# Rotary tables of a layer built by ScalarE in two slots, and the stream of groups written out without a loop

## The reference

```python
x = L0_attn_x
xn = _layernorm(x, axis=-1)
x = x + _L0_attn_ref(xn, ...) + _L0_ffn_ref(xn, ...)

# _L0_ffn_ref, DEPTH = 6
for i in range(DEPTH):
    x = attn_layer(shift_tokens(x), Wqkv[i], q_scale[i], k_scale[i], Wo[i]) + x
    x = ffn_layer(shift_tokens(x), ln_g[i], ln_b[i], W1[i], b1[i], W2[i], b2[i]) + x

# attn_layer: 16 heads of 64, windows of 32 tokens that see themselves and the window before
q = l2norm(q) * qs
k = l2norm(k) * ksc
q = q * cos * scale + rotate_half(q) * sin * scale
k = k * cos * inv + rotate_half(k) * sin * inv      # inv = 1 / scale
out = local_attention(q, k, v)
return out @ Wo
```

## Time and profile before

| | us |
|---|---|
| median of 3 runs | 2080.57 (2078.74 to 2081.38) |
| profiled execution, its own time | 2075.03 |
| its span, first to last instruction | 2073.2 |
| TensorE busy | 1919.3 (93%) |
| VectorE, ScalarE, GpSimd busy | 1605.8, 1390.0, 1341.2 |
| mean granted TensorE clock | 0.975 of full speed |

### The profile page before, as it was taken

How to read it: one execution, slowest core, us unless ns; L and a number is a source line. 1 busy time by engine, 2 the same in 40 slices (tenths; PEclk the granted TensorE clock), 3 DMA queues, 4 the chain that set the end, 5 groups by cost and what they waited for, 6 DMA issues and landing times. The chain is left out here.

```text
span 2073.2 us, 70057 instructions
## 1 busy us (share of the span) xinstructions
PE 1919.3 (93%) x26905; PEld 1408.2 (68%) x26905; DVE 1605.8 (77%) x3109; ACT 1390.0 (67%) x2780; POOL 1341.2 (65%) x1402
## 2 busy tenths in 40 slices
PE   4999997899999999989989999998999899999995
PEld 3667665777767767767767677676777676777762
DVE  5666665788898878888868988688888788888773
ACT  2665663677757767776767577676777675777762
POOL 0000004998788767878767977688878678787840
PEclk9999999999999999999999999999999999999996
DMA  2000000443424334333343243343333433333330
GB/s 95 2 1 0 0 30 6 115 107 101 123 76 105 96 92 119 90 90 96 98 112 100 75 104 98 90 121 88 91 100 96 116 93 79 103 99 96 98 91 20
DMA packets 190633, 171.70 MB, mean 83 GB/s; under 512 B 32160, under 2 KB 186440, under 8 KB 190152
## 3 DMA queue, kind: packets, MB, share of 16 engines
q1 hardware_dynamic: 190280, 167.02, 30.7%
HBM read 21.14 MB, written 1.05 MB: 11 GB/s over the span
## 5 line engine op out<-in xcount | busy, mean ns | idle before, releaser
L407 POOL TENSOR_TENSOR z_raw<-rot_u,rot_v 128x256 f32<-128x256 f32 x768 | 552.2, 743 | 186.3 <-DVE rot_v L1016 183.8
L422 POOL TENSOR_TENSOR z_norm<-probs_t,z_raw 128x512 f32<-128x512 f32 x384 | 493.1, 1306 | 110.4 <-DVE probs_t L1065 110.4
L1015 DVE TENSOR_TENSOR rot_u<-bank,tabs 128x512 f32<-128x512 f32 x384 | 263.1, 685 | 183.3 <-ACT sq L521 180.2
L781 PE MATMUL bank<-x_high,w_high 128*128 128x256 f32 x768 | 304.4, 396 | 2.8 <-issue 1.1
L553 ACT ACTIVATE pair_bank<-pair_bank 128x512 f32<-128x512 f32 x192 | 111.8, 582 | 256.1 <-DVE pair_bank L998 255.9
L521 ACT ACTIVATE sq<-bank 128x512 f32<-128x512 f32 x384 | 225.6, 589 | 53.9 <-PE bank L783 44.4
L1016 DVE TENSOR_TENSOR rot_v<-bank,tabs 128x512 f32<-128x512 f32 x384 | 261.5, 681 | 0.0
L428 POOL TENSOR_TENSOR sqs<-sq 128x512 f32<-128x512 f32 x192 | 245.3, 1278 | 23.6 <-POOL z_norm L422 23.5
L540 ACT ACTIVATE probs_t<-bank 64x512 f32<-64x512 f32 x384 | 227.3, 592 | 45.4 <-PE bank L760 43.1
L772 PEld LDWEIGHTS bank<-probs_t,v_late 128*64 128x64 f32 x3072 | 155.5, 138 | 145.8 <-issue 145.8
L825 PE MATMUL bank<-sqs,consts 128*128 128x512 f32 x384 | 204.4, 614 | 44.5 <-POOL sqs L428 41.5
(11 more groups left out here) (153 smaller groups left out, 4545.4 us busy)
## 6 DMA issues: line engine op xcount, KB each, us to landing
zqk<-z_norm SPq DMA_DIRECT2D x1536, 64.0 KB, 2.1
v_late<-v_sb SPq DMA_DIRECT2D x192, 192.0 KB, 2.6
w_qkv<-in_L_ffn_Wqkv SPq DMA_DIRECT2D x18, 512.0 KB, 5.1
v_late<-v_sb SPq DMA_DIRECT2D x192, 32.0 KB, 2.2
wo<-in_L_ffn_Wo SPq DMA_DIRECT2D x24, 128.0 KB, 2.1
w<-in_L_ffn_W SPq DMA_DIRECT2D x12, 170.5 KB, 3.0
consts<-in_constants SPq DMA_DIRECT2D x1, 1088.0 KB, 5.1
w_qkv<-in_L_attn_w_kv_up SPq DMA_DIRECT2D x2, 512.0 KB, 6.3
```

The source lines that it names most:

```text
L407: a = pool.tensor_tensor(z_raw[:, parity, idx, half, :], rot_u[:, idx, half, :], rot_v[:, idx, 1 - half, :], ALU.add)
L422: a = pool.tensor_tensor(z_norm[:, parity, idx, :, :], rinv[:, idx, :].unsqueeze(1).broadcast_to([P, 2, T]), z_raw[:, parity, idx, :, :], ...
L781: pe.matmul(dst, w_high[:, j, cols], x_high[:, odd, :], start=True, stop=False)
L1015: dve.tensor_tensor(rot_u[:, idx, :, :], src, tabs[:, 2 * idx, :, :], ALU.mult)
```

## The change

ScalarE builds the tables instead of VectorE, with activations that multiply by a column of `par_rot`. It does so in two parts: k's tables in local slot 27, with the copies of the scales, and q's tables in local slot 28, in both behind the squares of k. `par_rot` gets two more columns with negated scales. VectorE waits for a part of the tables at the first group of each layer. The first layer's tables stand on ScalarE ahead of the stream. The stream is written out slot by slot, with constants for counts and layers; the helpers for the loop and the two semaphores that were only incremented (`room_met`, `split_begun`) go.

```diff
-FIRST, LOOP, LAST = -4, 16, GROUPS + 14
-TURNS = DEPTH - 1
+FIRST, LAST = -4, GROUPS + 14
...
-        par_rot = sb("par_rot", [P, LG])
+        par_rot = sb("par_rot", [P, LG + 2])
...
-        def stream(eng, slot):
-
-            for k in range(FIRST, LOOP):
-                slot(k, 0)
-            with eng.Fori(0, TURNS) as r:
-                for k in range(LOOP, LOOP + LAYER):
-                    slot(k, r)
-            for k in range(LOOP, LAST - TURNS * LAYER):
-                slot(k, TURNS)
...
+        def stream(slot):
+
+            for s in range(FIRST, LAST):
+                slot(s)
...
+        def layer_begun(s, at):
+
+            l, k = divmod(s - at, LAYER)
+            return l + 1 if k == 0 and 0 <= l < DEPTH - 1 else 0
...
-                if k == LAYER - 14:
-                    sp.wait_ge(S["split_done"], G * (r + 1))
-                    sp.sem_inc(S["room_met"], 1)
-                    qkv_weights(r + 1)
+                l = layer_begun(s, LAYER - 14)
+                if l:
+                    sp.wait_ge(S["split_done"], G * l)
+                    qkv_weights(l)
...
+            def rotary_scales(l):
+                act.activation(par_rot[:, 0:LG], pars[:, 0:LG, ds(l, 1)].rearrange("p n a -> p (n a)"), ACT.Copy)
+                act.activation(par_rot[:, LG:LG + 2], pars[:, Q2:LG:2, ds(l, 1)].rearrange("p n a -> p (n a)"), ACT.Copy, scale=-1.0).then_inc(S["rot_par_ready"], 1)
+
+            def rotary_tables(l, idx):
+
+                act.wait_ge(S["rot_par_ready"], l + 1)
+                for part, c2 in enumerate((2 * idx + 1, LG + idx)):
+                    j = 2 * idx + part
+                    for half, c in enumerate((2 * idx, c2)):
+                        m = act.activation(tabs[:, j, half, :], con("rot")[:, j * T:(j + 1) * T], ACT.Copy, scale=par_rot[:, c:c + 1])
+                m.then_inc(S[("q_tabs_ready", "k_tabs_ready")[idx]], 1)
...
                 if one:
                     squares(s + 4, "k_prod", B_K, 1, "k_square")
+                l = layer_begun(s, LAYER - 5)
+                if l:
+                    rotary_scales(l)
+                    rotary_tables(l, 1)
+                l = layer_begun(s, LAYER - 4)
+                if l:
+                    act.wait_ge(S["q_prod"], LAYER * l)
+                    rotary_tables(l, 0)
...
             gains(0)
             gate_biases(0)
+            rotary_scales(0)
+            rotary_tables(0, 1)
+            rotary_tables(0, 0)
             act.wait_ge(S["spread_zero"], 2)
...
                 dve.wait_ge(S[done], m + 1)
                 after(dve, taken, m)
+                if m % LAYER == 0:
+                    dve.wait_ge(S[("q_tabs_ready", "k_tabs_ready")[idx]], m // LAYER + 1)
...
-            def rotary_tables(l):
-                dve.tensor_copy(par_rot[:, :], pars[:, 0:LG, ds(l, 1)].rearrange("p n a -> p (n a)")).then_inc(S["rot_par_ready"], 1)
-                dve.wait_ge(S["rot_par_ready"], l + 1)
-                for j, (c1, sign) in enumerate(((Q1, 1), (Q1, -1), (K1, 1), (K1, -1))):
-                    for half in range(2):
-                        m = dve.tensor_scalar(tabs[:, j, half, :], con("rot")[:, j * T:(j + 1) * T], par_rot[:, c1 + half:c1 + half + 1],
-                                              float(sign if half else 1), ALU.mult, ALU.mult)
-                m.then_inc(S["tabs_ready"], 1)
-                dve.wait_ge(S["tabs_ready"], l + 1)
...
-                if not isinstance(r, int) and k == LAYER - 5:
-                    rotary_tables(r + 1)
-                if not isinstance(r, int) and k == LAYER + 15:
-                    out_biases(r + 1)
+                l = layer_begun(s, LAYER + 15)
+                if l:
+                    out_biases(l)
...
             dve.wait_ge(S["pars_ready"], 1)
-            rotary_tables(0)
             out_biases(0)
```

More of the change, by code:

```diff
@@ L324, in _, with slot @@
             qkv_weights(0)
[L326 to L330, removed]
+            def slot(s):
+                if active(s, -2, GROUPS - 2):
+                    g = (s + 2) % G
                     sp.wait_ge(S["zn_ready"], s + 3)
@@ L354, in slot @@
[L354 to L372, removed]
+                    out_weights(0, s + 1)
+                l = layer_begun(s, LAYER - 14)
+                if l:
+                    sp.wait_ge(S["split_done"], G * l)
+                    qkv_weights(l)
+                for g in range(G):
+                    l = layer_begun(s, LAYER - 1 + g)
+                    if l:
+                        sp.wait_ge(S["lwo_done"], s - 1)
+                        out_weights(l, g)
@@ L374, in _ @@
+            stream(slot)
             sp.wait_ge(S["scores_done"], GROUPS)
@@ L428, in slot @@
                     pool.tensor_tensor(sqs[:, :, :], sq[:, :, 0, :], sq[:, :, 1, :], ALU.add).then_inc(S["sums_ready"], 1)
[L429 to L436, removed]
+                    rotated(s + 4, s % 2, 0, "q_prod", "q_summed")
+                for g in range(G):
+                    l = layer_begun(s, LAYER - 7 + g)
+                    if l:
+                        pool.wait_ge(S["w_in"], 16 * 3 * (l + 1))
+                        pool.wait_ge(S["lv_done"], s + 4)
+                        split_weights(l, g)
             pool.wait_ge(S["pv_done"], STEPS)
@@ L442, in _ @@
                 split_weights(0, g)
-            stream(pool, slot)
+            stream(slot)
         @block.scalar
@@ L521, in squares, with slot @@
                 act.activation(sq[:, idx, :, :], src[:, :].rearrange("p (a t) -> p a t", a=2), ACT.Square).then_inc(S[mark], 1)
-            def slot(k, r):
-                s, g = LAYER * r + k, k % G
-                one, two = active(k, r, -4, GROUPS - 4), active(k, r, -3, GROUPS - 3)
-                three, four = active(k, r, 0, GROUPS), active(k, r, 1, GROUPS + 1)
-                normed = g == 0 and active(k, r, 2 * G, 2 * G + GROUPS)
+            def slot(s):
+                g = s % G
+                one, two = active(s, -4, GROUPS - 4), active(s, -3, GROUPS - 3)
+                three, four = active(s, 0, GROUPS), active(s, 1, GROUPS + 1)
+                normed = g == 0 and active(s, 2 * G, 2 * G + GROUPS)
                 if two:
-                    m, og, odd = s + 3, (k + 3) % G, (k + 3) // G % 2
+                    m, og, odd = s + 3, (s + 3) % G, (s + 3) // G % 2
                     act.wait_ge(S["lv_done"], m + 1)
@@ L604, in _ @@
             gate_biases(0)
+            rotary_scales(0)
+            rotary_tables(0, 1)
+            rotary_tables(0, 0)
             act.wait_ge(S["spread_zero"], 2)
-            stream(act, slot)
+            stream(slot)
         @block.tensor
@@ L899, in _ @@
                 pt_taken(STEPS - 1, h)
-            stream(pe, slot)
+            stream(slot)
             for p in range(PAIRS):
@@ L1036, in out_biases, with slot @@
                 dve.wait_ge(S["out_bias_ready"], l + 1)
-            def slot(k, r):
-                s, g = LAYER * r + k, k % G
-                one, two, three = active(k, r, -4, GROUPS - 4), active(k, r, -3, GROUPS - 3), active(k, r, 0, GROUPS)
-                if k % (2 * G) == 5 and mlp_active(k, r, 21):
-                    p, b = mlp_of(k - 21, r), 2 * ((k - 21) // (2 * G)) % NB
+            def slot(s):
+                g = s % G
+                one, two, three = active(s, -4, GROUPS - 4), active(s, -3, GROUPS - 3), active(s, 0, GROUPS)
+                if mlp_slot(s, 21):
+                    p = (s - 21) // (2 * G)
+                    b = 2 * p % NB
                     dve.wait_ge(S["mlp_done"], p + 1)
@@ L1098, in _ @@
             dve.wait_ge(S["pars_ready"], 1)
-            rotary_tables(0)
             out_biases(0)
             turn(causal, 0, ("post",))
-            stream(dve, slot)
+            stream(slot)
             dve.wait_ge(S["mlp_res"], MLPS)
```

193 lines of the change are left out of this document (99 added, 94 removed).

## The result

The changed kernel takes 2020.82 us (median of 4 runs, 2016.41 to 2025.17), the kernel before 2079.65 in the same session (2073.41 to 2081.38). The ratio is 0.9722, with a 95% interval of 0.9693 to 0.9752: 2.8% less time. The profiled execution took 2020.56 us, its span is 2018.7.

The account below looks back on a forecast made before the run. TensorE, busy 93% of the span, bounds the kernel, so gains come from its waits. 29.8 + 21.1 + 2.2 = 53.1 us off the profiled 2075.03 gives 2021.9; with 5.5 up to the median 2027.5, range 2010 to 2040.

Parts of the forecast that it names:

- The loop: Local slots 47 and 48: without the four jumps back, 95.13 us falls to 65.32, a gain of 29.8 us.
- the slots at the exit: Local slots 47 and 48 at the loop's exit, with no jump: 16.33 us, taken as the price of each written-out pair.
- The rest of the written-out code: Plain blocks of the stream: constants for registers and the dropped `sem_inc` gain nothing, bounds under 1 us in all.
- VectorE's tables in the layers: Blocks from local slot 24: without VectorE's tables five blocks fall from 373.72 to 352.65 us, a gain of 21.1.
- The tables on ScalarE: Slots 59 and 60: ScalarE gets 2.2 and 1.6 us more, covered by idles, price 0; 19 us if no cover held.
- The Trainium skill's rule: Multiplications belong on VectorE; by it alone the move costs 1 us per layer of engine time, which idles hide.
- The first layer: End of the causal stage: TensorE no longer idles for VectorE's last copy, gain 2.2 us, bounds 1.5 and 2.4.
- From profiled run to median: Whole kernel: the median lay 5.5 us above the profiled execution, and the same difference took 2021.9 to 2027.5.
- GpSimd not taking over: Blocks from local slot 24: GpSimd's backlog is absorbed, they fall to plain 66.6, gain 40.6, time 2008.0; chance 0.08.
- ScalarE as the wait: Local slots 27 to 29: TensorE idles for ScalarE, 1 to 3.8 us lost per layer, 2032 to 2046; chance 0.10.
- The edge not being the jump: Local slots 47 and 48: weights' loads and bias copy cause the loss, the 29.8 us stay, time 2057; chance 0.04.
- The slower case: Whole stream: straight code starves TensorE's queue in each slot; decides from 0.33 us per slot, 2107 at 0.5; chance 0.04.

Follow-up runs that it names:

- experiment 1: The kernel before with its loop written out on all five engines, tables still on VectorE; 2042.01 us against 2077.72, ratio 0.9826.
- experiment 3: The kernel before with the stream written out on all engines but TensorE, which keeps its loop of five turns; 2079.18 us in one run.
- experiment 5: The changed kernel plus, on TensorE alone, a two-turn loop around one semaphore increment at slots 48, 80, 112 and 144; 2025.9 us in one run.
- experiment 6: The changed kernel without GpSimd's splitting of the weights of layers 1 to 5, which use the first layer's; 2011.52 us in one run.
- experiment 7: The changed kernel without ScalarE building the tables of layers 1 to 5, which use the first layer's; 2019.0 us in one run.
- experiment 8: The changed kernel with ScalarE making each of the four pieces of k's tables twice in layers 1 to 5; 2024.88 us in one run.
- experiment 9: The changed kernel with the high part of the weight split moved from GpSimd to ScalarE for layers 1 to 5; 2006.44 us against 2074.09, ratio 0.9663.
- experiment 10: The kernel of experiment 9 with k's tables moved behind the squares of q on ScalarE; 2006.84 us against 2080.12, ratio 0.9658.

## Why the prediction was right

The forecast was faster, at 2027.5 us with a range of 2010 to 2040; 2020.82 was measured. For the profiled execution it was 2021.9, and 2020.56 was measured.

- **The loop**, 29.8 us: 29.65 measured, and experiment 1 shows it with the tables left alone (29.64). That the slots at the exit give the price of a jump-free pair held to 0.04 us per pair. The cause, the engines fetching their code after a far jump, was argued from two transfer rows. Experiments 3 and 5 support it, in that TensorE's loop alone costs it all and that a near jump costs a tenth, but leave it an argument by elimination. Not foreseen: the other engines' jumps cost half of it by themselves.
- **The rest of the written-out code**, nothing, with bounds of 1 us: about 1.6 us of gain, slightly outside. A plain block takes 66.52 in place of 66.63, and that is too small to give it a cause.
- **VectorE's tables in the layers**, 21.1 us: 20.83 measured, 19.77 over the whole stream with the loop kept. GpSimd took over as forecast. Slots 58 and 59 took 18.61 (18.68 said), slot 60 9.73 (9.54), slot 61 9.31 (9.34). Slot 60's error comes from GpSimd's own instructions, not from the chain: from L395 on they are without a gap. Experiments 6 and 7 show the cause from both sides: without the splits 3.06 of the 70.58 - 66.52 = 4.06 us go, without ScalarE's tables none.
- **The tables on ScalarE**, price 0: the block of the seventh kernel is 0.02 us shorter than the changed one's. The piece of 0.40 us was right (0.40; four in 1.70). TensorE waited 0.65 for xc2, inside the 0.9 I allowed. But the argument had a hole. I followed the delay forward to TensorE's next sums, two slots on, and put VectorE's rotation of q, 2 us later, aside as harmless. The way back to GpSimd leads through it: VectorE's next slot, with the bound of the norm in it, starts later. That the price stayed 0 was so partly by luck. Experiment 8 shows that the cover ends less than one more part of 1.6 us away; experiments 6, 9 and 10 show that ScalarE's delay is next in line, about 1 us per block, once GpSimd is lighter.
- **The Trainium skill's rule** (ScalarE: Activation LUTs, Rules for kernel authors), that a multiplication belongs on VectorE, was weighed and set aside. The runs show both sides: eight pieces take 3.30 us on ScalarE against 2.19 on an undisturbed VectorE, and yet the move gains 4 us per layer, because in the stream they took 7.31 there and stood on the path.
- **The first layer**, 2.2 us: 2.39 at slot 0. L971 follows the bias copy, as said.
- **From profiled run to median**, 5.5 us: this was the weakest step. The profiled execution of before lay 5.5 below the median of three runs; the changed kernel's lies 0.3 from its median. In other sessions the medians of before were 2074.09 to 2080.12. The difference was scatter, not a constant; without it the forecast is 2021.9, 1.1 us from the measured median. That closeness is in part luck too: the medians differ by 58.8 us, and the sum explains 53.
- **The rivals.** GpSimd not taking over (2008.0) needed blocks of 66.6: they are 70.6. ScalarE as the wait needed TensorE idle beyond what the sums' slack covers: experiment 7 refutes it. The edge not being the jump (2057) falls with experiment 1. The slower case falls with the plain blocks, which take 66.5 us in straight code (now all of slots -4 to 205, 210 slots and not 196). Their places were well chosen: the first comes out when the splits go, and the second is what then stops it.

## What to carry to other kernels

In a stream whose bound engine waits at a loop's edge, compare the slots across the jump with the same slots at the exit: the difference is what writing out gives, but only if every engine's loop goes, since their costs lie side by side. When work is taken off one engine, cost the stretch by the engine that is next in line (here GpSimd's 9.34 us period), and expect only what is over its time (here half of the excess) to come back. An engine with idle time covers a move only up to the first result that others wait for behind it, and a delay is to be followed all the way round, back to the engine that is the bound.

## What the runs showed of the hardware

**The end of the kernel varies by itself.** Behind slot 184 all kernels do the same work, yet that stretch takes 105.0 to 114.0 us, with the granted clock. Rows of experiments 1 and 3, then of the kernel before:

```profile
1932.60:2037.64 105.04, 78.16 (x971) 47.47 (x969) 57.90 (x99) 53.65 (x86) 28.98 (x31) 0.91 0.23 61
```

```profile
1963.41:2077.39 113.98, 88.28 (x971) 50.07 (x969) 57.74 (x99) 53.76 (x86) 28.99 (x31) 0.81 0.21 56
```

```profile
1964.22:2073.21 108.99, 82.92 (x971) 48.31 (x969) 57.77 (x99) 53.73 (x86) 29.01 (x31) 0.85 0.22 59
```

VectorE's, ScalarE's and GpSimd's busy times agree within 0.2 us; TensorE's does not (78.16, 88.28, 82.92), and its clock is at the lower of its two levels, 1.2 GHz, for some 18, 44 and 33 us of it. TensorE has long waits there, since few groups are left. The twelve profiled executions line up: the three of 105 us have 18 us at the lower clock, those of 112.5 to 114 have 41 to 44. Such 9 us are as large as the spread of the runs of one kernel; that they make up most of it is argued, not shown.

**The same work has another price beside GpSimd.** VectorE's eight table pieces take 2.19 us alone and 7.31 in the stream, while ScalarE's take 3.30 in the one and 3.41 in the other. Within one stretch of the kernel before the pieces part by what GpSimd does. The sixth of them runs beside GpSimd's L400 (881.38 to 883.19), and the last two after it, when GpSimd idles:

```profile
881.37 1.97 DVE L1029 TENSOR_SCALAR tabs<-consts,par_rot 128x256 f32<-128x256 f32 x1
...
883.26 0.60 DVE L1029 TENSOR_SCALAR tabs<-consts,par_rot 128x256 f32<-128x256 f32 x2
```

**A far jump costs 7.4 us on the path and a near one 0.73.** Behind the far one TensorE also dropped to half clock for a while (0.86 granted over the pair); behind the near one it did not.
